# Expert slots in halves of 322 and 320 columns instead of 324, and the mixer's values in banks of the ring

## Time and profile before

| | |
|---|---|
| runs | 695.46, 697.65, 701.62 us, median 697.65 |
| profiled execution | 699.12 us, its span 697.4 us |
| TensorE | busy 608.8 us, 87% of the span, 4100 matmuls |
| DVE, ACT, GpSimd | busy 498.6, 352.9, 334.2 us |
| granted TensorE clock | 0.926 in the mean |
| queue of GpSimd's DMAs | 9216 packets, 7.8% of 16 engines |

### The profile page before, as it was taken

One profiled execution on the slowest core, in us unless ns is written; L12 is line 12 of the kernel. 1 busy time (PEld: TensorE's weight loads), 2 busy tenths in 40 slices (PEclk: granted clock), 3 DMA queues, 4 the chain that ended last, 5 costly groups with the idle time before them and its releaser, 6 DMA issues.

```text
span 697.4 us, 11909 instructions
## 1 busy us (share of the span) xinstructions
PE 608.8 (87%) x4100; PEld 506.9 (73%) x4100; DVE 498.6 (71%) x1066; ACT 352.9 (51%) x685; POOL 334.2 (48%) x322
## 2 busy tenths in 40 slices
PE   3787998998989789899998725999999999999992
PEld 2666887787877545555564425999999999999991
DVE  6887687787688867678874442778787888788740
ACT  4774563663552333363534213566666666656551
POOL 1065324324340013331535464446776868686776
PEclk9897999999999989999987655999999999999997
DMA  8302306765338745955735006223626262621224
GB/s 281 119 31 43 109 31 160 258 180 150 92 93 226 170 112 139 240 147 155 191 117 184 23 15 199 99 86 91 163 41 179 27 178 30 172 32 14 26 33 45
DMA packets 63317, 81.65 MB, mean 117 GB/s; under 512 B 10296, under 2 KB 47939, under 8 KB 63257
## 3 DMA queue, kind: packets, MB, share of 16 engines
q1 hardware_dynamic: 53928, 72.85, 36.8%
q0 software_dynamic: 9216, 7.81, 7.8%
q10 hardware_dynamic: 112, 0.23, 0.1%
HBM read 48.27 MB, written 34.36 MB: 118 GB/s over the span
## 4 chain that ended last, share of the span: by engine, by line
PE 42%; DVE 5%; issue 4%; POOL 4%; DMA 4%; ACT 3%; ACTq 0%; SPq 0%; DVEq 0%; POOLq 0%
PE l_scores L101 13%; PE l_turned L1900 7%; PE l_out L1900 3%; PE l_shared L1900 3%; PE l_turned L340 2%; POOL out L1604 2%; ACT l_area L370 2%; PE l_scores L1834 2%; PE l_turned L324 2%; PE l_out L360 2%; PE l_shared L1776 2%; DMA l_q_more<-md 1%; PE l_scores L1857 1%; DMA l_hi<-md 1%; PE l_scores L265 1%
## 5 line engine op out<-in xcount | busy, mean ns | idle before, releaser
L2089 DVE SCALAR_TENSOR_TENSOR w_v<-w_th,l_scores 128x324 f32<-128x324 f32 x128 | 62.2, 490 | 55.0 <-ACT w_th L1691 53.7
L1691 ACT ACTIVATE w_th<-l_scores 128x324 f32<-128x324 f32 x128 | 56.4, 441 | 83.4 <-PE l_scores L101 82.1
L1591 POOL TENSOR_TENSOR l_lo<-w_v,l_hi 128x324 fp32r<-128x324 f32 x64 | 59.0, 922 | 74.6 <-ACT l_hi L1697 74.4
L370 ACT ACTIVATE l_area<-l_turned 128x1024 f32<-128x1024 f32 x48 | 49.1, 1023 | 82.4 <-PE l_turned L340 79.6
L101 PE MATMUL l_scores<-l_hi,w_w1h 128*128 128x324 f32 x256 | 81.0, 316 | 2.3 <-DVE l_lo L2081 1.2
L1604 POOL DMA_INDIRECT out<-l_area,w_to x48 | 76.3, 1591 | 12.0 <-issue 9.7
L101 PE MATMUL l_scores<-l_lo,w_w1h 128*128 128x324 f32 x256 | 80.3, 314 | 0.0
L101 PE MATMUL l_scores<-l_hi,w_w1l 128*128 128x324 f32 x256 | 80.1, 313 | 0.0
L294 DVE TENSOR_REDUCE l_nm<-l_scores 128x4 f32<-128x1024 f32 (+1 forms) x45 | 54.7, 1215 | 19.8 <-PE l_scores L280 19.6
L1697 ACT ACTIVATE l_hi<-w_v 128x324 fp32r<-128x324 f32 x128 | 59.9, 472 | 12.4 <-DVE w_v L2089 11.8
L2063 DVE TENSOR_TENSOR w_w2l<-w_s,w_w2h 128x256 fp32r<-128x256 f32 x56 | 60.9, 1088 | 1.9
(11 more groups left out here) (459 smaller groups left out, 1715.4 us busy)
## 6 DMA issues: line engine op xcount, KB each, us to landing
w_s<-in_L_ffn_w SPq DMA_DIRECT2D x14, 1024.0 KB, 7.4
disp<-c_blank SPq DMA_DIRECT2D x8, 658.1 KB
l_lo<-kd SPq DMA_DIRECT2D x26, 200.0 KB
l_hi<-qd SPq DMA_DIRECT2D x26, 192.0 KB
w_rows<-disp SPq DMA_DIRECT2D x7, 658.1 KB
kd<-l_qkh SPq DMA_DIRECT2D x16, 256.0 KB, 4.7
vd<-l_area SPq DMA_DIRECT2D x4, 1024.0 KB, 6.5
qd<-l_qkh SPq DMA_DIRECT2D x16, 256.0 KB, 4.2
```

The lines of the kernel that those rows point to most:

```text
L370: act.activation(lead.pr[n % 3][:, :], lead.tbank[:, :], ACT.Exp, scale=SCALE).then_inc(A["exp"], 1)
L1591: pool.tensor_tensor(hl[:, g % 3, half(1)], v[:, n % 4, :], hh[:, g % 3, half(1)].bitcast(F32), ALU.subtract)\
L1691: act.activation(th[:, n % 2, :], hb[n % 2][:, 0:HALF], ACT.Tanh, scale=0.5).then_inc(F["th"], 1)
L2089: dve.scalar_tensor_tensor(v[:, n % 4, :], th[:, n % 2, :], 1.0, hb[n % 2][:, 0:HALF], ALU.add, ALU.mult).then_inc(F["v"], 1)
```

## The change

**Experts.** Tile `t` is worked only in the rows that it can have filled, `USED = (107, 107, 108, 107, 107, 106)`: the third and the sixth are made one row wider where the sum of three would be odd. The two halves are `WIDTH = (322, 320)` columns, and tiles start in a half at `AT`. All transposes, products, copies and scatters of the experts take these widths; the table in DRAM and the places of the halves in SBUF stay.

**Mixer.** The values' products go to banks 0 and 1 of the ring (behind `dl` 3 and `A` 3, which were there) instead of a pair of their own. `PAIRS` has ten names, and the C products come in the pair behind K, which is the one that `w3` used. The waits follow: `values` waits for the DVE's reading of `A` 3 instead of `x_out` and `dx`; `mixed` waits for `x_out` and `dx` instead of `kl`; `turn_q` and `turn_x` wait for `kl` instead of `vf`; the chunks `dl` 0 and `A` 0 of the next iteration wait for `vf` too, as does unit 0 of the attention; the last `w2` does not.

```diff
+USED = [-(-(CAP - t) // ST) for t in range(ST)]
+USED = [w + (sum(USED[t - ST // 2 + 1:t + 1]) % 2 if t % (ST // 2) == ST // 2 - 1 else 0) for t, w in enumerate(USED)]
+WIDTH = (sum(USED[0:ST // 2]), sum(USED[ST // 2:ST]))
+AT = [t // (ST // 2) * HALF + sum(USED[t // (ST // 2) * (ST // 2):t]) for t in range(ST)]
...
-PAIRS = ("Q", "T", "D", "W1", "W2", "TC", "W3", "K", "V", "C", "TQ")
+PAIRS = ("Q", "T", "D", "W1", "W2", "TC", "W3", "K", "C", "TQ")
...
                 def turn_x(i):
-                    ge(pe, S["vf"], 2 * (i - 1))
+                    ge(pe, S["kl"], DC * (i - 1))
...
                 def turn_q(i):
-                    pe.wait_ge(S["vf"], 2 * upto(i + 2))
+                    pe.wait_ge(S["kl"], DC * upto(i + 2))
...
                 def chunk(i, name, m):
+                    if name in ("dl", "A") and m == 0:
+                        ge(pe, S["vf"], 2 * (i - 1) + (1 if name == "dl" else 2))
...
                 def mixed(i, m):
-                    pe.wait_ge(S["kl"], DC * (i + 1))
+                    pe.wait_ge(S["dx"], DC * (i + 1))
+                    ge(pe, S["x_out"], 2 * i)
...
                 def w2(i):
-                    if i == NBLK - 1:
-                        pe.wait_ge(S["vf"], 2 * NBLK)
-                    else:
+                    if i < NBLK - 1:
                         ge(pe, S["ql"], DC * i)
...
                 def values(i):
-                    ge(pe, S["x_out"], 2 * i)
-                    pe.wait_ge(S["dx"], DC * (i + 1))
+                    pe.wait_ge(S["ring"], made(i, "A", 3))
...
-                            mm = split_product(pe, pair(i, "V", n)[:, j * D:(j + 1) * D],
+                            mm = split_product(pe, banks[n][:, j * D:(j + 1) * D],
...
                     if u == 0:
                         pe.wait_ge(S["ring"], 12 * NBLK)
+                        pe.wait_ge(S["vf"], 2 * NBLK)
...
-                        ins = dve.tensor_tensor(v_rows(n, s), v_heads(pair(i, "V", n), s), v_heads(bv, s), ALU.add)
+                        ins = dve.tensor_tensor(v_rows(n, s), v_heads(banks[n], s), v_heads(bv, s), ALU.add)
...
-        def half(n):
-            return slice(n * HALF, (n + 1) * HALF)
+        def half(n, u):
+            return slice(n * HALF, n * HALF + WIDTH[u])
...
-                        out=out, out_offset=bass.IndirectOffsetOnAxis(ap=to[:, e % 3, t:t + 1], axis=0),
-                        in_=y[e % 2][:, t, :], in_offset=None, bounds_check=N + SLOTS - 1, oob_is_err=True,
+                        out=out, out_offset=bass.IndirectOffsetOnAxis(ap=to[0:USED[t], e % 3, t:t + 1], axis=0),
+                        in_=y[e % 2][0:USED[t], t, :], in_offset=None, bounds_check=N + SLOTS - 1, oob_is_err=True,
...
-                    for t in range(3):
-                        mm = pe.transpose(tb[n % 2][:, t * SP_:(t + 1) * SP_], rows[e % 2][:, 3 * f + t, k * P:(k + 1) * P],
-                                          c["ident"][0:SP_, 0:SP_])
+                    for t in range(3 * f, 3 * f + 3):
+                        at, w = AT[t] - AT[3 * f], USED[t]
+                        mm = pe.transpose(tb[n % 2][:, at:at + w], rows[e % 2][0:w, t, k * P:(k + 1) * P], c["ident"][0:w, 0:w])
...
-                    split_product(pe, hb[n % 2][:, 0:HALF],
+                    split_product(pe, hb[n % 2][:, 0:WIDTH[u]],
...
-                                    mm = pe.matmul(eb[2 * k + u][:, 0:HALF], w2_piece(w, f)[:, k * P:(k + 1) * P], a[:, g % 3, half(q)],
+                                    mm = pe.matmul(eb[2 * k + u][:, 0:WIDTH[u]], w2_piece(w, f)[:, k * P:(k + 1) * P], a[:, g % 3, half(q, u)],
```

More of the change, by code:

```diff
@@ L1423, in w2_piece, with spot @@
             return m[:, f * D:(f + 1) * D]
-        def half(n):
-            return slice(n * HALF, (n + 1) * HALF)
+        def half(n, u):
+            return slice(n * HALF, n * HALF + WIDTH[u])
+        def spot(n):
+            e, r = divmod(n, 2 * FC)
+            return (e, r // 2, r % 2) if e < E - 1 else (e, r % FC, r // FC)
         def w2_done(f):
@@ L1590, in low @@
                     pool.wait_ge(F["hh"], n + 1)
-                    pool.tensor_tensor(hl[:, g % 3, half(1)], v[:, n % 4, :], hh[:, g % 3, half(1)].bitcast(F32), ALU.subtract)\
+                    pool.tensor_tensor(hl[:, g % 3, half(1, spot(n)[2])], v[:, n % 4, 0:WIDTH[spot(n)[2]]],
+                                       hh[:, g % 3, half(1, spot(n)[2])].bitcast(F32), ALU.subtract)\
                         .then_inc(F["hl_odd"], 1)
@@ L1685, in turned @@
                     ge(act, F["h"], HU * (e - 1))
-                    act.activation(xh[e % 2][:, k, half(f)], tb[n % 2][:, 0:HALF], ACT.Copy).then_inc(F["xh"], 1)
+                    act.activation(xh[e % 2][:, k, half(f, f)], tb[n % 2][:, 0:WIDTH[f]], ACT.Copy).then_inc(F["xh"], 1)
                 def silu(n):
@@ L1690, in silu @@
                     ge(act, F["v"], n - 1)
-                    act.activation(th[:, n % 2, :], hb[n % 2][:, 0:HALF], ACT.Tanh, scale=0.5).then_inc(F["th"], 1)
+                    act.activation(th[:, n % 2, 0:WIDTH[spot(n)[2]]], hb[n % 2][:, 0:WIDTH[spot(n)[2]]], ACT.Tanh, scale=0.5).then_inc(F["th"], 1)
                 def high(n):
@@ L1696, in high @@
                     ge(act, F["r"], g - 2)
-                    act.activation(hh[:, g % 3, half(u)], v[:, n % 4, :], ACT.Copy).then_inc(F["hh"], 1)
+                    act.activation(hh[:, g % 3, half(u, spot(n)[2])], v[:, n % 4, 0:WIDTH[spot(n)[2]]], ACT.Copy).then_inc(F["hh"], 1)
                 def result_out(e, u):
@@ L1701, in result_out @@
                     ge(act, F["yt"], 3 * e)
-                    act.activation(yt[:, 0, half(u)], eb[u][:, 0:HALF], ACT.Copy).then_inc(F["ye_act"], 1)
+                    act.activation(yt[:, 0, half(u, u)], eb[u][:, 0:WIDTH[u]], ACT.Copy).then_inc(F["ye_act"], 1)
                 def result(e, t):
@@ L1876, in hidden @@
                     ge(pe, F["v"], n - 1)
-                    split_product(pe, hb[n % 2][:, 0:HALF],
+                    split_product(pe, hb[n % 2][:, 0:WIDTH[u]],
                                   [((w1h[:, k * FF + f * P:k * FF + (f + 1) * P], w1l[:, k * FF + f * P:k * FF + (f + 1) * P]),
-                                    (xh[e % 2][:, k, half(u)], xl[e % 2][:, k, half(u)])) for k in range(DC)])\
+                                    (xh[e % 2][:, k, half(u, u)], xl[e % 2][:, k, half(u, u)])) for k in range(DC)])\
                         .then_inc(F["h"], 1)
@@ L2080, in turned @@
                     dve.wait_ge(F["xh"], TU * e + n + 1)
-                    dve.tensor_tensor(xl[e % 2][:, k, half(f)], tb[n % 2][:, 0:HALF], xh[e % 2][:, k, half(f)].bitcast(F32),
+                    dve.tensor_tensor(xl[e % 2][:, k, half(f, f)], tb[n % 2][:, 0:WIDTH[f]], xh[e % 2][:, k, half(f, f)].bitcast(F32),
                                       ALU.subtract).then_inc(F["xl"], 1)
@@ L2094, in low @@
                     dve.wait_ge(F["hh"], n + 1)
-                    dve.tensor_tensor(hl[:, g % 3, half(0)], v[:, n % 4, :], hh[:, g % 3, half(0)].bitcast(F32), ALU.subtract)\
+                    dve.tensor_tensor(hl[:, g % 3, half(0, spot(n)[2])], v[:, n % 4, 0:WIDTH[spot(n)[2]]],
+                                      hh[:, g % 3, half(0, spot(n)[2])].bitcast(F32), ALU.subtract)\
                         .then_inc(F["hl"], 1)
@@ L2100, in result_out @@
                     ge(dve, F["yt"], 3 * e)
-                    dve.tensor_copy(yt[:, 1, half(u)], eb[2 + u][:, 0:HALF]).then_inc(F["ye_dve"], 1)
+                    dve.tensor_copy(yt[:, 1, half(u, u)], eb[2 + u][:, 0:WIDTH[u]]).then_inc(F["ye_dve"], 1)
                 def result(e, t):
```

17 lines of the change are left out of this document (8 added, 9 removed).

## The result

The changed kernel takes 806.69 us in the median of 4 runs (804.38 to 811.21); the kernel before, run on the same chip beside it, 696.56 (693.43 to 701.62). The ratio is 1.1625, with a 95% interval of 1.1571 to 1.168: slower by 110 us, where 690.0 was forecast with a range to 695.7. The rival that had the sign right, scatters on one engine, had a chance of 0.04 and a price of 6.6 us.

The account below looks back on a forecast made before the run. TensorE's streamed columns were taken to bound the experts, a loop of late TensorE and idle DVE the mixer's boundaries. 699.12 - 5.6 (mixer) - 2.1 (experts) = 691.4, on the median 690.0 us; range 687.2 to 695.7.

Parts of the forecast that it names:

- scatters on one engine: Rival, experts: 107-row scatters go out in line on one DMA engine, landing late; +6.6 us, 704 in all; chance 0.04.
- the narrower columns: Experts: 768 hidden and 768 result products lose 4608 columns in all at 0.45 ns each; 2.1 us saved.
- the rule: Experts' scatters: a DMA splits over the largest number up to 16 dividing its rows: 108 on 12 engines, 107 on one.
- The share of 0.90: DMA engines' mean share at 689.5 to 690 before, 108-row scatters alone; held against the rule, as 12 of 16 give 0.75.
- the wait for expert 6's rows: Priced within the one-engine rival: GpSimd waits near the end for that expert's late-landing rows; 6.5 us more.
- the mechanism: Mixer iteration ends: values skip the residual wait, C products and turn start earlier, idle DVE time goes; 5.6 us saved.
- The added waits: Mixer: next iteration's two chunks, C products and attention's unit 0 wait for more; costed at nothing, 0.6 us at most for the chunks.
- the clock takes it back: Rival, mixer: TensorE's clock falls behind new idle times before `queries` in iterations 2 and 3; +3.4 us, 693.4; chance 0.15.
- cover: Experts: narrower copies on ACT, DVE and GpSimd lie beside TensorE's products; losing that cover would save, not cost.

Follow-up runs that it names:

- the experiment with cut rows: Probably the kernel before with an expert's six scatters giving 96, 104, 105, 98, 102 and 100 rows in place of 108; one execution, 700.96 us.

## Why the prediction was wrong

**The step that failed** is the scatter of 107 rows, costed at "between 0 and 1.58/108 = 15 ns" saved, and with it the rival's weight. It costs 2.58 us more of GpSimd each, and its rows land 15 to 20 us after the start in place of 4. With 108 rows in the scatters the total comes out (689.34 against 690.0), but in part by luck: the mixer alone measured 1.9 us faster (ratio 0.9973) and not 5.6, the narrower columns show 0.5 us in the profile and not 2.1, and the kernel with 112 rows, whose scatters are cheaper still, is 2.5 to 6.8 us faster than before and not 7.7.

*The evidence against the rule was read too strongly.* The share of 0.90 was taken as a count of engines. At the end of the kernel with the sixth scatter at 107 rows, one such scatter is alone under way, and from 751 on only its rows are left:

```profile
751.00:756.00 5.00, 0.00 (x0) 0.00 (x0) 0.00 (x0) 0.00 (x0) 0.00 (x0) 0.50 0.08 12
```

(us, five engines, clock, DMA share, GB/s.) The share is 0.08, or 1.3 engines, while 12 GB/s are 12 rows a us, one behind the other. Packets of an engine overlap, so the share overstates its engines: by this figure, an estimate, 12 engines can show 12 x 0.08 = 0.96, and the 0.90 says nothing against them. The row that would have settled it was on record: 312 small packets beside 648 rows make 160 a scatter, 16 x 10 and not 16 x 8 as rows spread over all 16 would give; but that sum is known only now.

*The rival was priced at the end only.* +6.6 us took two late landings. It left out GpSimd's own time (some 73 us, which no row of before could show, and which therefore wanted a wide bound) and that each of six more experts begins with a wait for all rows of the one before (most of the other 37 us). The text had the wait for expert 6's rows and didn't ask for the other experts, whose first scatter comes 12 us after the last one of the expert before:

```profile
528.41 1.58 POOL L1604 DMA_INDIRECT out<-l_area,w_to  x1 [0.19 <-issue]
...
540.37 1.58 POOL L1604 DMA_INDIRECT out<-l_area,w_to  x1 [0.19 <-issue]
```

That covers a landing after 4 us and not one after 19.

*Mixer: the mechanism was right.* After's timelines of the DVE and TensorE answer to the earlier trace rows:

```profile
116.20 1.26 DVE L1186 TENSOR_TENSOR_SCAN m_ssm<-l_turned,m_dx 128x256 f32<-128x256 f32 x2
117.38 0.66 DVE L1100 TENSOR_TENSOR m_xal<-l_out,m_xah 128x512 fp32r<-128x512 f32 x1
...
118.56 1.26 DVE L1186 TENSOR_TENSOR_SCAN m_ssm<-l_turned,m_dx 128x256 f32<-128x256 f32 x2
```

```profile
109.32 0.47 PE L105 MATMUL l_turned<-m_gh,l_hi 128*128 128x512 f32 x1 [0.36 <-issue]
...
119.96 0.47 PE L105 MATMUL l_turned<-m_xah,m_wh 128*128 128x512 f32 x1 [1.11 <-DVE m_ssm L1186]
```

C starts at 109.32 (109.25 forecast), the low part of x2 at 117.38 without idle time (119.81 before), the second sum ends at 119.82 (119.9), and `queries` start after 1.11 us (1.3). The added waits cost nothing. The mixer's end, the attention's unit that waits for the last sum, comes at 214.68, where it came at 220.00: 5.3 us, for 5.6 forecast.

*Its size hangs on the execution that it is measured against.* In the experiment with cut rows the mixer is that of before, and the clock stayed up. First its DVE's timeline, then its busy time in two stretches (columns as above, with busy us and counts of five engines), then one of these stretches in the execution of before:

```profile
118.40 0.69 DVE L1096 TENSOR_TENSOR m_xal<-l_out,m_xah 128x512 fp32r<-128x512 f32 x1 [0.84 <-ACT m_xah L738]
```

```profile
104.00:120.00 16.00, 13.66 (x75) 11.40 (x74) 13.70 (x33) 6.32 (x12) 7.72 (x6) 1.00 0.52 125
...
215.00:220.00 5.00, 3.27 (x23) 2.37 (x24) 4.87 (x8) 1.64 (x4) 0.00 (x0) 1.00 0.98 298
```

```profile
104.00:120.00 16.00, 13.68 (x69) 11.69 (x68) 12.17 (x31) 4.91 (x9) 7.69 (x6) 0.89 0.53 128
```

After the same idle 2.3 us the clock fell in one execution (0.89 over 104 to 120) and not in the other, and the DVE's idle time is 0.84 us, not 2.37. That execution is at the attention's unit by 217.23; the change is worth 2.6 us against it. The other kernels bear this out. The old mixer reaches the unit at 220.0 to 220.4 in three executions with 0.89 over 104 to 120, and at 217.2 to 218.6 in five with 1.00; the new mixer at 214.0 to 214.7 in all four, with 1.00. So about half of the 5.3 us is a fall of the clock that the kernel before has in some executions, and that none of the four with the shorter idle time has. And the rival *the clock takes it back* came true at a place that I hadn't looked at. TensorE's timeline and the busy time of after, at that unit:

```profile
214.68 0.39 PE L269 MATMUL l_turned<-c_mask,c_identb 128*128 128x256 bf16 x2 [2.60 <-DVE m_ssm L1186]
```

```profile
215.00:220.00 5.00, 5.00 (x18) 3.91 (x18) 4.57 (x6) 2.60 (x3) 0.00 (x0) 0.66 0.83 222
```

With the DVE late, TensorE is idle for 2.60 us ahead of it (1.73 before), and the clock behind is 0.66 over 215 to 220, in the mixer alone too (0.66) and with 108 and 112 rows (0.50 and 0.66), and 1.00 in all eight executions with the old mixer. Both together fit the measured 0.9973 better than 5.6 us do.

*Experts' columns: price right, cover wrong.* 0.45 ns a column is confirmed by the run with 300 columns, but the 2.1 us are not there in full. With 108 rows the experts' stretch (420.2 to 672.4) is 0.5 us shorter than before, and with 112 rows (418.9 to 670.3) 1.3 us: differences that single executions can just show. The timelines say why the steps differ, 3.57 us from scatter to scatter with 108 rows (518.54 to 522.11), 3.54 with 112:

```profile
518.54 1.58 POOL L1616 DMA_INDIRECT out<-l_area,w_to  x1 [0.19 <-issue]
520.10 0.93 POOL L1602 TENSOR_TENSOR l_lo<-w_v,l_hi 128x320 fp32r<-128x320 f32 x1
...
522.11 1.58 POOL L1616 DMA_INDIRECT out<-l_area,w_to  x1 [0.19 <-issue]
```

```profile
517.25 1.47 POOL L1616 DMA_INDIRECT out<-l_area,w_to  x1 [0.16 <-issue]
518.87 0.88 POOL L1602 TENSOR_TENSOR l_lo<-w_v,l_hi 128x320 fp32r<-128x320 f32 x1 [0.15 <-ACT l_hi L1709]
...
520.79 1.46 POOL L1616 DMA_INDIRECT out<-l_area,w_to  x1 [0.16 <-issue]
```

With 108 rows GpSimd has no idle time before its low part and sets the step; with 112 it waits for ACT again, and TensorE does.

**Open.** With one slow scatter an expert, the landing beside the weights' loads takes 4.8 us more than alone. How much of the 19 us in the changed kernel is contention with them, and how much other scatters on the same engine, was not separated. It was not settled whether 112 rows beat 108 in time. Why the forecast total was met with 108 rows while its parts measured less stays open too; the spread of the runs would allow it.

## What to carry to other kernels

Keep the row count of an indirect scatter at a multiple of 16 or of a number a little below it, and pad the rows rather than cut them; here one row less in a scatter cost 2.58 us of GpSimd and, in an expert's sixth scatter, a landing five times as late. An engine whose idle time lies in other steps than its load is at its bound in the loaded steps, however its mean share looks. When a rival can't be refuted by a row that says exactly that, follow it through every place where the operation stands, and give its unknown price the whole range.

## What the runs showed of the hardware

- A scatter with added rows issues 16 x (rows / k + 1) packets, k the largest divisor of the rows up to 16, and takes GpSimd 1.3 us + 1.65 ns a packet: 1.46 us for 96 rows, 1.47 for 112, 1.58 for 108, 1.76 for 102, 2.72 for 106, 4.16 for 107.
- 107 rows of 1 KB in line landed 11.7 us after the end of the issue when alone, at 12 rows a us once they flowed, and 16 beside the weights' loads.
- GpSimd's next instructions run while such an issue goes on, but take 2.7 us in place of 0.9 each.
- The mean share of DMA engines counts overlapping packets: one engine's rows showed as 0.08 of 16, or 1.3 engines.
- After the same 2.3 us of idle TensorE the clock fell in three executions of the same mixer (0.89 over 104 to 120) and not in five others (1.00), which goes with 2.8 us by the attention's unit that waits for the last sum (220.00 against 217.23).
